# A ViT tower on one core: attention scores from round-mode products over doubled heads, and a new order of the image stage

## The reference

```python
gray = jnp.einsum('bchw,c->bhw', x, w)[:, None]
edges = jax.lax.conv_general_dilated(gray, scharr, ...)
edge = jnp.sqrt(jnp.square(edges)).sum(axis=1) / 2
...
x_proj = jax.nn.silu(x @ W1 + b1)
u, v, q, k = jnp.split(x_proj, 4, axis=-1)
scores = jnp.einsum('bqhd,bkhd->bhqk', qh, kh)      # 16 heads, d = 16
attn = jax.nn.silu(scores) / S
av = jnp.einsum('bhqk,bkhd->bqhd', attn, vh).reshape(B, S, D)
y = _layernorm(av * u, gamma, beta) @ W2 + b2
...
h = h + y; xf = _layernorm(h)                        # then statistics of xf, router, experts
```

## Time and profile before

| | |
|---|---|
| median of three runs | 1576.35 us (1574.70 to 1579.21) |
| the profiled execution | 1575.64 us, its span 1573.9 us |
| busy over the span | PE 1357.2, DVE 1042.5, ACT 904.5, POOL 418.8 us |
| mean granted clock of TensorE | 0.924 of full speed |

### The profile page before, as it was taken

One profiled execution on the slowest core, in us unless ns is written; L12 is line 12 of the kernel. 1 busy time (PEld: TensorE's weight loads), 2 busy tenths in 40 slices (PEclk: granted clock), 3 DMA queues, 4 the chain that ended last, 5 costly groups with the idle time before them and its releaser, 6 DMA issues. The chain is left out here.

```text
span 1573.9 us, 32849 instructions
## 1 busy us (share of the span) xinstructions
PE 1357.2 (86%) x12092; PEld 1063.4 (68%) x12092; DVE 1042.5 (66%) x2696; ACT 904.5 (57%) x1628; POOL 418.8 (27%) x434
## 2 busy tenths in 40 slices
PE   3899999999999999999984723339999999999996
PEld 1566666666666666666653713229999999999996
DVE  4356666566666666666644487887777777777774
ACT  1577777777777777777762215344455555455552
POOL 0112212122121221212201000013555554545553
PEclk8899999999999999999996555579999999999999
DMA  7324435334243342443203330005565655556552
GB/s 225 100 77 120 119 82 133 102 99 132 76 126 108 93 133 80 121 113 88 65 28 108 114 3 0 1 9 186 145 193 150 185 167 169 172 164 184 151 162 26
DMA packets 128869, 177.33 MB, mean 113 GB/s; under 512 B 19994, under 2 KB 117164, under 8 KB 124652
## 3 DMA queue, kind: packets, MB, share of 16 engines
q1 hardware_dynamic: 111340, 154.45, 32.5%
q0 software_dynamic: 17408, 21.25, 8.4%
HBM read 134.24 MB, written 41.41 MB: 112 GB/s over the span
## 5 line engine op out<-in xcount | busy, mean ns | idle before, releaser
L682 ACT ACTIVATE at<-ps_s 128x1024 f32<-128x1024 f32 x256 | 248.8, 1028 | 42.7 <-PE ps_s L561 42.7
L202 PE MATMUL ps_s<-xet,whi 128*128 128x322 f32 x640 | 205.7, 321 | 12.4 <-issue 10.9
L1869 POOL DMA_INDIRECT out_rows<-ye,slot_token x96 | 153.4, 1598 | 225.4 <-ACT ye L1714 215.0
L203 PE MATMUL ps_s<-xet,wlo 128*128 128x322 f32 x640 | 199.9, 312 | 0.0
L204 PE MATMUL ps_s<-xet,whi 128*128 128x322 f32 x640 | 198.7, 311 | 0.0
L1683 ACT ACTIVATE sg<-ps_s 128x322 f32<-128x322 f32 x160 | 70.4, 440 | 176.8 <-PE ps_s L204 126.0
L1784 DVE TENSOR_TENSOR wlo<-raw,whi 128x640 fp32r<-128x640 f32 x192 | 154.0, 818 | 2.3 <-ACT whi L1693 1.3
L561 PE MATMUL ps_s<-q,k 32*128 32x256 f32 x2048 | 146.6, 400 | 1.4 <-ACT at L682 1.4
L577 PE MATMUL ps_av<-at,uv 128*16 128x257 f32 x2048 | 136.0, 383 | 0.3 <-ACT at L740 0.3
L202 PEld LDWEIGHTS ps_s<-xet,whi 128*128 128x128 f32 x640 | 121.3, 190 | 20.6 <-issue 20.0
L202 PE MATMUL ps_av<-whi,hs 128*128 128x256 f32 (+1 forms) x480 | 134.4, 280 | 0.8 <-DVE wlo L1784 0.5
(11 more groups left out here) (357 smaller groups left out, 3367.8 us busy)
## 6 DMA issues: line engine op xcount, KB each, us to landing
raw<-in_wexp SPq DMA_DIRECT2D x32, 1280.0 KB, 6.3
halo<-gray_dram SPq DMA_DIRECT2D x96, 288.0 KB
xb<-in_x SPq DMA_DIRECT2D x64, 384.0 KB, 5.1
raw<-in_wexp SPq DMA_DIRECT2D x32, 640.0 KB
gray_dram<-g SPq DMA_DIRECT2D x32, 256.0 KB, 3.2
out_rows<-h SPq DMA_DIRECT2D x64, 128.0 KB, 6.8
token_rows<-xf SPq DMA_DIRECT2D x64, 128.0 KB, 4.2
pre_dram<-pre SPq DMA_DIRECT2D x32, 128.0 KB, 5.1
```

What stands on the lines that cost most here:

```text
L202: nc.tensor.matmul(o, lh, rh, start=first, stop=False)
L203: nc.tensor.matmul(o, ll, rh, start=False, stop=False)
L682: nc.scalar.activation(at[:, t, 2 * i:2 * i + 2, :, 0:R].rearrange("p j k q -> p (j k) q"), ps_s[i][:, :, :, :].rearrange("p j k q -> p (j ...
L1869: nc.gpsimd.indirect_dma_start(out=out, out_offset=bass.IndirectOffsetOnAxis(ap=slot_token[0:w, 3 * m + st:3 * m + st + 1], axis=0), in_=y ...
```

## The change

Scores. q and k are now written once each by ScalarE (`qn`, `kn`). VectorE doubles every head with `stream_shuffle`, which moves rows within strips of 32: `dup[:, par]` holds the 16 rows of the even (`par = 0`) or the odd head in both halves of a strip. For q, ScalarE rounds the 1024 columns to fp32r (`hi_q`) and VectorE takes the remainder (`split_q`), both into `qd`. For k, VectorE rounds `dup` into `kd` and then overwrites it by `kd * CUP + dup`, where `CUP` is 0 on the first 16 rows of a strip and -1 on the others: the first half holds rounded k, the second its remainder (`stack_k`). A product of such a strip with rounded q, plus one with q's remainder, gives the score of one head. `score(t)` therefore has 16 fp32r matmuls where it had 8 plain ones. `cls_scores` reads `qn` and `kn`, and has 4 plain matmuls where it had 6.

Order. All bodies are written in a new order, and `UNITS`, `READ` and `LAG` follow. The transposition of xf and the whole router work of an image (units F0 and G0) now belong to image `e`, a step later than before for F0. Gray images are made for `gm = n+4`. SyncE asks for the shifted copies behind the gray store and the load of x, after a wait for the convolution that read the buffer.

```diff
-            c[32 * j + 16 * par:32 * j + 16 * par + 16, CE2 + par] = 1
+    c[:, CUP] = -(p // 16 % 2)
...
-        q2 = [s1(f"q2{i}", [P, 2, D]) for i in range(2)]
-        k2 = [s1(f"k2{i}", [P, 2, 2, D]) for i in range(2)]
+        qn = s1("qn", [P, 2, D])
+        kn = s1("kn", [P, 2, D])
+        dup = s1("dup", [P, 2, 2, D])
+        qd = [s1(f"qd{i}", [P, 2, 2, 2, D], f32r) for i in range(2)]
+        kd = [s1(f"kd{i}", [P, 2, 2, D], f32r) for i in range(2)]
...
-        UNITS = ["B0", "A0", "E", "D0", "D1", "G0", "B1", "D2", "A1", "D3", "B2", "B3", "B4", "D4"]
+        UNITS = ["A0", "B0", "D0", "D1", "E", "F0", "B1", "D2", "B2", "A1", "B3", "D3", "G0", "B4"]
...
             def score(n, r, m, t):
                 if t == 0:
-                    pe.wait_ge(qk_act, 2 * m + 2)
+                    pe.wait_ge(q_ready, m + 1)
+                    pe.wait_ge(k_ready, m + 1)
...
-                    for j in range(4):
-                        last = nc.tensor.matmul(ps_s[j // 2][:, j % 2, kt, :], k2[r % 2][32 * j:32 * j + 32, e, a, kt * 128:kt * 128 + 128],
-                                                q2[r % 2][32 * j:32 * j + 32, a, :], start=True, stop=True)
+                    for hl in range(2):
+                        for j in range(4):
+                            row = slice(32 * j, 32 * j + 32)
+                            last = nc.tensor.matmul(ps_s[j // 2][:, j % 2, kt, :], kd[r % 2][row, e, a, kt * 128:kt * 128 + 128],
+                                                    qd[r % 2][row, hl, e, a, :], start=hl == 0, stop=hl == 1)
...
+                def hi_q():
+                    act.wait_ge(q_dup, b + 1)
+                    wait(act, scores, 4 * (b - 1))
+                    nc.scalar.activation(qd[(r + 1) % 2][:, 0, :, :, :].rearrange("p e t q -> p (e t q)"),
+                                         dup[:, :, :, :].rearrange("p e t q -> p (e t q)"), ACT.Copy).then_inc(q_hi, 1)
...
+                def shuffled(src, ready, done):
+                    dve.wait_ge(qk_act, ready)
+                    nc.vector.memset(spare[:, :], 0.0)
+                    for par in range(2):
+                        half = [16 * par + i for i in range(16)]
+                        last = nc.vector.stream_shuffle(dup[:, par, :, :].rearrange("p t q -> p (t q)"),
+                                                        src[:, :, :].rearrange("p t q -> p (t q)"), half + half)
+                    last.then_inc(done, 1)
...
+                def stack_k():
...
+                    nc.vector.tensor_copy(flat_k, flat_d).then_inc(k_hi, 1)
+                    dve.wait_ge(k_hi, b + 1)
+                    nc.vector.scalar_tensor_tensor(flat_k, flat_k.bitcast(f32), cst[:, CUP:CUP + 1], flat_d,
+                                                   ALU.mult, ALU.add).then_inc(k_ready, 1)
...
-                a, b, c, d, e, gm = n + 2, n + 1, n, n - 1, n - 2, n + 3
+                a, b, c, d, e, gm = n + 2, n + 1, n, n - 1, n - 2, n + 4
...
                 if grayed(gm):
+                    sp.wait_ge(conv_done, 2 * (gm - 1))
                     load_halo(sp, gm)
```

More of the change, by code:

```diff
@@ L538, in cls_scores @@
                 bank_free(pe, n, "E")
+                pe.wait_ge(qk_act, 2 * m + 2)
                 for a in range(2):
[L540 to L544, removed]
+                    nc.tensor.matmul(bank("E")[32 * a:32 * a + 32, 0:R], cw[:, a, :], qn[:, a, :], start=True, stop=True)
+                for a in range(2):
+                    last = nc.tensor.matmul(bank("E")[64 + 32 * a:96 + 32 * a, 0:R], cw[:, 2 + a, :], kn[:, a, :], start=True, stop=True)
                 last.then_inc(cls_ps, 1)
             def cls_turn(m):
+                pe.wait_ge(cls_act, m + 1)
+                wait(pe, av_out, 4 * m)
                 mine = ps_av[1][:, 320:448].rearrange("p (c k) -> p k c", k=2)
@@ L624, in body @@
                     score(n, r, c, 0)
-                if has(a):
-                    conv(n, r, a, 0, "A0")
+                if has(d):
+                    back(n, r, d, 0)
+                    back(n, r, d, 1)
                 if has(c):
@@ L629, in body @@
                     score(n, r, c, 1)
[L630 to L633, removed]
+                if has(e):
+                    transposes(n, "F0", xf, xf_done, e + 1, xft_ps)
                 if has(c):
                     cls_turn(c)
[L636 to L639, removed]
                 if has(b):
                     proj_qk(n, b, 0, "B1")
[L642 to L643 removed]
                 if has(c):
@@ L647, in body @@
                     transposes(n, "D2", z, z_done, d + 1, zt_ps)
+                if has(b):
+                    proj_qk(n, b, 1, "B2")
                 if has(c):
+                    weighted(n, r, c, 1)
                     score(n, r, c, 2)
@@ L699, in silu_k @@
                     act.wait_ge(qk_ps, 2 * b + 2)
+                    wait(act, k_dup, b)
+                    wait(act, cls_ps, b)
                     for t in range(2):
-                        for par in range(2):
-                            last = nc.scalar.activation(k2[(r + 1) % 2][:, par, t, :], bank("B2")[:, 256 * t:256 * t + 256], ACT.Silu,
-                                                        bias=bk4[:, 2 * par + t:2 * par + t + 1], scale=cst[:, CE2 + par:CE2 + par + 1])
+                        last = nc.scalar.activation(kn[:, t, :], bank("B2")[:, 256 * t:256 * t + 256], ACT.Silu,
+                                                    bias=b1qk_sb[:, 2 + t:3 + t])
@@ L762, in body @@
                 if has(c):
-                    av_copy(1)
-                if has(b):
-                    silu_k()
-                if has(c):
-                    silu_scores(3)
+                    silu_scores(2)
+                    av_copy(0)
+                if has(e):
+                    stats_hi()
                 if has(b):
@@ new lines, in keep_class @@
+                def keep_class():
+                    dve.wait_ge(av_out, 4 * c + 4)
+                    nc.vector.tensor_copy(clsav[:, :, c], avs[:, :, R]).then_inc(cls_kept, 1)
+                if has(a):
+                    edges(0)
+                if has(b):
+                    turned_lo(xt, bank("B0")[:, :], xt_hi, b, xt_done)
+                if has(d):
+                    gated(0)
+                if has(e):
+                    most()
+                if has(d):
+                    gated(1)
@@ new lines, in body @@
+                if has(e):
+                    least()
+                if has(d):
+                    stats_z()
+                if grayed(gm):
+                    gray_green(dve, gm)
+                if has(e):
+                    turned_lo(xft, bank("F0")[:, :], xft_hi, e, xft_done)
+                if has(d):
+                    norm_z()
+                if grayed(gm):
+                    gray_blue(dve, gm)
+                if has(b):
+                    double_q()
+                if has(e):
+                    last_stats()
@@ L884, in body @@
+                if has(d):
+                    turned_lo(zt, bank("D2")[:, :], zt_hi, d, zt_done)
+                if has(b):
+                    split_q()
+                    double_k()
+                if has(a):
+                    edges(1)
                 if has(b):
@@ L927, in body @@
                     rsqrt("z", ve_z, rs_z, d)
-                if has(d):
-                    wait(pool, xf_done, d)
-                    rsqrt("h", ve_h, rs_h, d)
                 if has(a):
```

238 lines of the change are left out of this document (134 added, 104 removed).

## The result

| | before | changed |
|---|---|---|
| median of four runs | 1576.84 us (1574.70 to 1579.21) | 1501.88 us (1500.34 to 1505.52) |
| ratio, 95% interval | | 0.9528 (0.9505 to 0.9550) |
| profiled execution, its span | 1575.64, 1573.9 us | 1505.52, 1503.7 us |
| PE, DVE, ACT, POOL busy over the span | 1357.2, 1042.5, 904.5, 418.8 us | 1297.0, 1213.2, 891.3, 451.1 us |
| one step of the image stage | 24.42 us | 21.85 us |

The kernel became 75 us faster. The prediction said 54, and the time lies 7 us under the low end of its range. The profiled execution of the changed kernel was the slowest of its four, so lengths are taken from the step and not from the span.

What follows compares the result with a forecast made beforehand. TensorE's list bounds the step (24.06 of 24.42 us busy). List 22.03 plus idle 0.5 gives 22.5, 1.9 less; 29 steps give 55 us, the ends 2, less 3 for later start and tail: 54 us, 1523; range 1509 to 1572.

Steps and rivals of the forecast that it cites:

- Score pieces: TensorE, four per step: round-mode groups 0.115 us apart make a piece 0.67 instead of 1.07 us, 1.60 less per step.
- Class scores: TensorE's cls_scores: from four plain groups to two, 1.00 us less 2 x 0.216, so 0.43 less per step.
- ScalarE: ScalarE's work per step, with fewer writes of k and the added rounding of q: 17.7 us, hidden under TensorE.
- VectorE's sum: VectorE's work per step: 15.46 plus 5.5 us for doubling, splitting and stacking, 21.0 in all, 1.0 less than TensorE.
- my own row: Shuffle of 512 columns on VectorE, taken as 0.69 us like most other 512-column operations there.
- VectorE's loop: Loop through VectorE and TensorE closed at k_ready, 21.3 us; as rival bound: step 23.3, 1547 us, chance 0.17.
- The failed step: TensorE's new order: moving units removes nothing, each tiling change costs 0.2 us, their number stays; idle 0.5 instead of 0.36.
- The ends: Image stage's ends: three less full steps give 2 us; later first scores cost 2 us, the last image's norm 1.
- VectorE as the bound: Rival: VectorE or its loop bounds the step through slow shuffles or added waits; step 23.3, 1547 us, chance 0.17.
- Pieces no shorter: Rival on TensorE: score groups start no faster than 0.216 us, only the class scores gain; 1567 us, chance 0.10.
- strips that take turns: Rival on TensorE: round-mode strips not side by side, piece 2.05 us, 1680; chance 0.15 together with very slow shuffles.

Runs made afterwards that it cites:

- The first experiment: Changed kernel with each score piece again 8 plain f32 matmuls and the product with q's remainder left out: 1552.77 us, ratio 0.9850, step 23.43.
- the same move: Kernel before with k's projection directly behind the gate's second projection: 1579.22 us alone; 1572.09 us with ScalarE's copy of the second edges also ahead of the third score silu.

## Why the prediction was too cautious

**Score pieces: right.** 0.67 us predicted and measured, groups 0.117 apart. The first experiment puts their effect at 1.57 us a step. The Trainium skill's floor of about 25 ns between starts ("TensorE: Matmul & The Clock Gate", section "Wait — 56ns, not 53.3ns?") is kept by the 28 and 29 ns here. Its 62 ns per matmul, which it states for hardware decode switched off, did not show: 32 records in a row went at 28 ns each; no run shows which way they are decoded.

**Class scores: right.** 0.57 us; two groups less at 0.216.

**ScalarE: right.** 17.55 us against 17.7, hidden.

**VectorE's sum: right, from two errors.** 20.73 us against 21.0. The shuffles took 743 to 758 ns and not 690, k's last operation 1285 and not 1220. By the distance of their starts the new operations take 1.33, 1.30, 1.28 and 1.91 us (the two pairs of shuffles, the split, the two that stack k), 5.8 in all and not 5.5. But the engine's busy time rose by only 5.27, so the operations that were there before now count for 0.5 us less; I read that as more overlap in a list with fewer gaps. The Trainium skill's mode for the shuffle ("VectorE: DVE Perf Modes", section "The perf-mode tier table") gave an estimate of 0.79, nearer than my own row.

**VectorE's loop: the length right, but it isn't the only one.** I had 21.3 us for a loop closed at k_ready. Lengthening VectorE showed a floor of 21.85 - 0.51 = 21.3 us, with the waits at z and at the remainder of z; in the full steps TensorE never waited at k_ready. The list between y and z with GpSimd's reciprocal root in it was judged covered and wasn't counted as a loop.

**The failed step: "Moving units around removes nothing, but each change of tiling costs its 0.2 us, and their number stays about the same", and behind it "I put the idle of a step at 0.5 us instead of 0.36".** These two are one error, to treat the new order as a cost only. Predicted 22.5, measured 21.85: 0.65 us a step and 19 us over 29 steps, of the 21 us by which the time was missed. 0.5 of it is the idle, put at 0.5 without a sum behind it and measured as none: the order takes the wait for y out (0.30 of the 0.36 us before). The rest is the list, put at 22.03 and measured at 21.85. The number of changes did stay about the same (18 and 19), but one price for all of them was wrong: z's transposition ahead of k's projection saves 0.18, the second projection between another projection and the statistics saves 0.18, the last weighted piece ahead of a convolution about 0.1, against 0.36 more in the gate with the turned class weights and 0.11 more in the projections. The ledger has 0.16 us saved on balance, 0.52 with the idle; the order alone, with the old products, measured 0.61.

**The ends: mis-sized, and they cancel.** The first gate came 3.5 us later, not 2, and the tail grew by 0.6 and not 1. The ends gave 3.0 us, not 2: 77.2 less 29 x 2.56. Another 2 us came from outside the image stage, where I had put nothing, and no run says from what.

**The range.** Its low end, 1509, is about the sum with no idle at all in a list of 22.03 us: 2.38 x 29 + 2 - 3 = 68 us less. So it allowed for the idle to go, and not for the list itself to be shorter than 22.03. It is 21.85, and 0.18 x 29 = 5 us of the 7 below the range are this shorter list, to which I had given no bound.

**The rivals.** VectorE as the bound: no, but it is half a microsecond away. Pieces no shorter, and strips that take turns: refuted by the group distance of 0.117.

## What to carry to other kernels

When a change rewrites the order of a list that sets the pace, price each unit by its new neighbours from rows that have such a pair, beside the waits that the order adds and removes, and bound both sums on both sides; the number of changes alone said nothing here. A reorder is worth something only together with the reader of the bank that it needs: the same move gave +0.06 us a step alone and -0.12 with one ScalarE copy moved ahead. To find how much room the next engine has, lengthen it: several slacks in one trace can be the same to 10 ns, and the instruction that waits is then the first behind the added work. And read a lengthened kernel step by step, since a longer wait can cost TensorE its clock and so more than itself.

## What the runs showed of the hardware

- Four round-mode matmuls in four 32-row strips lie side by side: a group takes 0.117 us at 256 columns. At 128 columns it is still 0.110.
- In this kernel 16 round-mode records with 256 columns are faster than 8 plain matmuls of the same shape (0.67 against 1.07 us for a piece), since each plain one leaves two records at 54 ns each.
- A shuffle of 128x512 f32 on VectorE takes 743 to 758 ns, 0.06 to 0.07 us more than the two-source f32 operations of that size here (685 ns).
- TensorE's granted clock fell to 1.2 GHz in three of 26 full steps that all have a wait of about 1.9 us, and came back within the step; such a step is 1.5 us longer. With waits of 0.68 us it did not fall.
- The price of a change between forms of matmul is paid on both sides. The second projection's twelve records take 1.59 us between a convolution and the weighted values, and 1.41 between a projection and a transposition. Its first two records before, behind the convolution, and then in the changed kernel:

```profile
408.71 0.38 PE L202 MATMUL ps_f<-w2s,zt 128*128 128x256 f32 x1
408.93 0.28 PE L203 MATMUL ps_f<-w2s,zt 128*128 128x256 f32 x1
```

```profile
404.21 0.28 PE L201 MATMUL ps_f<-w2s,zt 128*128 128x256 f32 x1
404.33 0.28 PE L202 MATMUL ps_f<-w2s,zt 128*128 128x256 f32 x1
```

The first distance is 0.22 us and the second 0.12: 0.1 us for coming out of 32-wide weights, and about as much again where the next part has another form. The same 128 rows and columns are not enough for this: k's projection behind z's transposition still has 0.21 us between its first two records.

```profile
398.44 0.37 PE L201 MATMUL ps_f<-xt,w1s 128*128 128x256 f32 x1
398.65 0.28 PE L202 MATMUL ps_f<-xt,w1s 128*128 128x256 f32 x1
```
